# Layer 2's expert blocks: gate and up weights held on TensorE, the turned rows stream

## The reference, cut to what matters

```python
h = silu(einsum('nd,ehd->neh', flat, gate_w)) * einsum('nd,ehd->neh', flat, up_w)
expert_out = einsum('neh,edh->ned', h, down_w)
sel = take_along_axis(expert_out, topk_idx[:, :, None], axis=1)
out = (sel * topk_scores[:, :, None]).sum(axis=1)
out = out + silu(flat @ sgate_w.T) * (flat @ sup_w.T) @ sdown_w.T
```

## Time and profile before

| | |
|---|---|
| median of 3 runs | 3837.25 us (3829.97 to 3837.67) |
| profiled execution | 3835.66 us, its span 3833.8 us |
| the blocks' stretch | first gather at 2457.8 us, last copy of Y at 2690.4 us, next stage from 2693.5 us |
| granted TensorE clock | 0.962 over the span |

### The profile page before, as it was taken

One profiled execution on the slowest core, in us unless ns is written; L12 is line 12 of the kernel. 1 busy time (PEld: TensorE's weight loads), 2 busy tenths in 40 slices (PEclk: granted clock), 3 DMA queues, 4 the chain that ended last, 5 costly groups with the idle time before them and its releaser, 6 DMA issues. The chain is left out here.

```text
span 3833.8 us, 90102 instructions
## 1 busy us (share of the span) xinstructions
PE 3465.1 (90%) x30069; PEld 2574.1 (67%) x30069; DVE 2688.0 (70%) x5870; ACT 2437.2 (64%) x9595; POOL 2075.0 (54%) x2606
## 2 busy tenths in 40 slices
PE   8989979988988999999889998899899998788897
PEld 5656645557776878888666665666688874456587
DVE  6857749977774767777688886644577754979822
ACT  6958944445452437777635991455688875688655
POOL 4534319977993433344366540275666635556744
PEclk9989999999999999999989998999999999999889
DMA  7013420010000000000000003135500003300078
GB/s 110 2 23 48 53 61 1 1 56 1 1 1 22 2 2 7 6 7 6 6 2 6 12 7 119 28 99 91 220 22 21 22 30 116 116 2 10 31 263 302
DMA packets 320103, 185.17 MB, mean 48 GB/s; under 512 B 214104, under 2 KB 289127, under 8 KB 318613
## 3 DMA queue, kind: packets, MB, share of 16 engines
q1 hardware_dynamic: 303716, 147.68, 14.2%
q0 software_dynamic: 13568, 27.36, 3.1%
q10 hardware_dynamic: 2370, 4.39, 0.3%
HBM read 131.43 MB, written 50.54 MB: 47 GB/s over the span
## 5 line engine op out<-in xcount | busy, mean ns | idle before, releaser
L3889 POOL DMA_INDIRECT l2f_b_xb<-l2f_tokens,l2f_inv x160 | 155.5, 972 | 174.8 <-issue 157.9
L2684 POOL TENSOR_TENSOR l1x_Sx<-l1x_Sx,l1x_sm 128x512 f32<-128x512 f32 x128 | 132.6, 1046 | 184.7 <-DVE l1x_sm L2890 184.7
L2684 POOL TENSOR_TENSOR l3a_Sx<-l3a_Sx,l3a_sm 128x512 f32<-128x512 f32 x128 | 133.4, 1043 | 129.8 <-DVE l3a_sm L2890 128.2
L3005 ACT ACTIVATE l1x_Sx<-l1x_Sx,l1x_nmx 128x128 f32<-128x128 f32 x512 | 199.0, 393 | 3.8 <-DVE l1x_nmx L2884 3.8
L1470 PEld LDWEIGHTS l0f_acc<-l0f_d_xk,l0f_d_Z 128*128 128x128 f32 x1024 | 124.7, 191 | 113.8 <-POOL l0f_d_Z L1438 112.8
L3005 ACT ACTIVATE l3a_Sx<-l3a_Sx,l3a_nmx 128x128 f32<-128x128 f32 x512 | 199.0, 392 | 0.1
L865 ACT ACTIVATE l3f_Pr<-l3f_S,l3f_nmx 128x128 f32<-128x128 f32 x512 | 182.5, 402 | 3.3 <-DVE l3f_nmx L795 3.3
L865 ACT ACTIVATE l2x_Pr<-l2x_S,l2x_nmx 128x128 f32<-128x128 f32 x512 | 183.9, 426 | 0.4 <-DVE l2x_nmx L795 0.4
L1350 ACT ACTIVATE l0x_Pr<-l0x_S,l0x_nmx 128x128 f32<-128x128 f32 x512 | 181.4, 403 | 3.1 <-DVE l0x_nmx L1267 2.6
L865 ACT ACTIVATE l0a_Pr<-l0a_S,l0a_nmx 128x128 f32<-128x128 f32 x512 | 182.6, 406 | 0.7 <-DVE l0a_nmx L795 0.7
L1470 PE MATMUL l0f_acc<-l0f_d_xk,l0f_d_Z 128*128 128x128 f32 x1024 | 144.5, 284 | 25.1 <-POOL l0f_d_Z L1438 24.9
(11 more groups left out here) (757 smaller groups left out, 11938.7 us busy)
## 6 DMA issues: line engine op xcount, KB each, us to landing
l3f_b_W<-in_l3f_we SPq DMA_DIRECT2D x72, 514.0 KB, 5.5
l3f_sorted<-l3a_blank SPq DMA_DIRECT2D x1, 17680.0 KB, 51.1
l3x_Mb<-l3x_dram_max SPq DMA_DIRECT2D x32, 512.0 KB, 4.3
l2f_results<-l2f_b_ys SPq DMA_DIRECT2D x40, 256.0 KB, 2.8
l2f_W<-in_l2f_w SPq DMA_DIRECT2D x1, 6144.0 KB, 25.9
l3f_b_xb<-l3f_sorted SPq DMA_DIRECT2D x72, 65.0 KB, 4.4
l0f_ew<-in_l0f_ew SPq DMA_DIRECT2D x1, 4096.0 KB, 13.2
l3f_XS<-l3f_results SPq DMA_DIRECT2D x8, 512.0 KB, 6.6
```

Source lines behind the costliest of these rows:

```text
L2684: pool.tensor_tensor(quad(Sx, s, q), quad(Sx, s, q), bcast_in(sm[:, s, 4 * q:4 * q + 4], P), ALU.mult).then_inc(w_done, 1)
L3005: ins = nc.scalar.activation(Sx[:, s, h, :], Sx[:, s, h, :], ACT.Exp, bias=nmx[:, s, h:h + 1], accum_out=sm[:, s, h:h + 1])
L3889: pool.indirect_dma_start(xb[:, j % 16, :], None, rows[:, :], bass.IndirectOffsetOnAxis(inv[:, j:j + 1], 0), bounds_check=None).then_inc(x ...
```

## The change

The operands of G change places. A ring `wst` of 3 is added in SBUF, 128 x 256 each. VectorE gets a step `weights`: it reads `owner` into a register of its own, and copies the block's gate and up columns into the ring. TensorE holds the ring's gate part, then its up part, and `xT` streams, 128 columns each time, so that G has the hidden width on the partitions. `h` then already lies as `down` needs it: H, its copy, its PSUM bank and `hT` are left out. `product` of block j, which writes `h[j % 2]`, waits for Y of block j-2 where it waited for H of block j-2. `weights` of block j+3 stands ahead of the product of block j+2 in VectorE's loop.

```diff
+        wst = sb("wst", [P, 3, 2 * P])
         h = sb("h", [P, 2, P])
-        hT = sb("hT", [P, 2, P])
...
                 def hidden(j):
-                    if j == blocks - 1:
-                        wait(pe, xt_done, j + 1)
-                    nc.tensor.matmul(G[j % 2][:, 0:2 * P], xT[:, j % 2, :], columns[:, bass.ds(at[j % 4], 2 * P)],
+                    wait(pe, w_done, j + 1)
+                    wait(pe, xt_done, j + 1)
+                    nc.tensor.matmul(G[j % 2][:, 0:P], wst[:, j % 3, 0:P], xT[:, j % 2, :],
+                                     start=True, stop=True)
+                    nc.tensor.matmul(G[j % 2][:, P:2 * P], wst[:, j % 3, P:2 * P], xT[:, j % 2, :],
                                      start=True, stop=True).then_inc(u_mm, 1)
 
-                def turn_hidden(j):
+                def down(j):
                     wait(pe, h_done, j + 1)
-                    wait(pe, ht_done, j)
-                    nc.tensor.transpose(H[:, 0:P], h[:, j % 2, :], C.ident).then_inc(ht_mm, 1)
-
-                def down(j):
-                    if j == blocks - 1:
-                        wait(pe, ht_done, j + 1)
                     wait(pe, y_done, j)
-                    nc.tensor.matmul(Y[:, 0:P], hT[:, j % 2, :], columns[:, bass.ds(at[j % 4] + 2 * P, P)],
+                    nc.tensor.matmul(Y[:, 0:P], h[:, j % 2, :], columns[:, bass.ds(at[j % 4] + 2 * P, P)],
                                      start=True, stop=True).then_inc(y_mm, 1)
...
-                    if 0 <= j + 1 < blocks:
-                        turn_hidden(j + 1)
                     if j >= 0:
                         down(j)
...
                 def product(j):
                     wait(dve, silu_done, j + 1)
-                    wait(dve, ht_mm, j - 1)
+                    wait(dve, y_mm, j - 1)
                     nc.vector.tensor_tensor(h[:, j % 2, :], sg[:, j % 2, :], G[j % 2][:, P:2 * P], ALU.mult).then_inc(h_done, 1)
-
-                def copy_hidden(j):
-                    wait(dve, ht_mm, j + 1)
-                    wait(dve, y_mm, j - 1)
-                    nc.vector.tensor_copy(hT[:, j % 2, :], H[:, 0:P]).then_inc(ht_done, 1)
...
+                def weights(j):
+                    at = dve.value_load(owner[0:1, j:j + 1], min_val=0, max_val=(experts - 1) * width)
+                    wait(dve, u_mm, j - 2)
+                    nc.vector.tensor_copy(wst[:, j % 3, :], columns[:, bass.ds(at, 2 * P)]).then_inc(w_done, 1)
+
+                weights(0)
                 for j in range(-2, blocks):
+                    if j + 3 < blocks:
+                        weights(j + 3)
...
                     if j + 2 < blocks:
                         product(j + 2)
-                    if 0 <= j + 1 < blocks:
-                        copy_hidden(j + 1)
```

More of the change, by code:

```diff
@@ L3871, in gathered_blocks @@
         nth, mine = [sb(nm, [P, NB, experts]) for nm in ("nth", "mine")]
-        T, H, Y, Gs, Us, Ys = [ps(nm) for nm in ("T", "H", "Y", "Gs", "Us", "Ys")]
+        T, Y, Gs, Us, Ys = [ps(nm) for nm in ("T", "Y", "Gs", "Us", "Ys")]
         G = [ps("G0"), ps("G1")]
-        (xt_mm, xt_done, u_mm, silu_done, h_done, ht_mm, ht_done, y_mm, y_done, masked, counted, picked, gu_mm,
-         gate_done, hs_done, ys_mm, xs_done) = sems(17)
+        (xt_mm, xt_done, u_mm, silu_done, h_done, y_mm, y_done, masked, counted, picked, gu_mm,
+         gate_done, hs_done, ys_mm, xs_done, w_done) = sems(16)
         x_in = C.l2f_taken
```

## The result

The kernel after took 3858.42 us (median of 5 runs, 3856.57 to 3859.40) beside 3837.67 us for the kernel before (5 runs, 3829.97 to 3845.99): ratio 1.0051, 95% interval 1.0039 to 1.0062, which is 15 to 24 us slower. The forecast was 3862, in a range of 3840 to 3886.

The account below looks back on a forecast made before the run. TensorE's instruction stream, 1.16 us per block, was taken as the bound; a new ring of 1.39 per block adds +3.4 (last 16), +1.3 (first 18) and +21.5 (middle), +26.2 on 3835.66: 3861.9 us, range 3840 to 3886.

Parts of the forecast that it names:

- The ring: Y(j-2) to product, weights copy, G(j) and Y(j): 2.77 us for two blocks, 1.39 per block; 3862, chance 0.62.
- Y's tail: Ring link on TensorE from Y's weight load to its records' end: 0.49 us.
- Product to copy: Ring link on VectorE, product's start to weights copy's start: 0.95 us, 0.65 for the read and 0.3 for address and waits.
- From the copy's end to Y's weight load: Ring link: 0.12 to wake TensorE and load G's weights, 0.79 with the address load, 0.10 for Y's waits and address.
- Y's end to the product: Ring link from the end of Y(j-2) to the start of product(j): 0.04 us.
- The sum: Added time over the expert blocks: last 16 +3.4, first 18 intervals +1.3, middle +21.5 with nine of eleven paying; together +26.2 us.
- TensorE's own stream after: TensorE's instruction stream without H's turn, if nothing else held it: 1.06 to 1.10 us per block.
- the faster rival: VectorE's address read hides behind the wait for Y(j-2), so no ring limits the blocks: 3827, chance 0.12.
- The port: VectorE's weights copies and GpSimd's gathers hold each other up: 0.00 to 0.05 us per copy counted, at most 0.31.
- the third rival: Port conflict on every weights copy: +0.31 us on the ring, +18 us on top, 3880; chance 0.12.
- The clock: TensorE, less busy, drops to 1.2 GHz, adding some 0.6 us to the ring: +35 us, 3897; chance 0.04.
- the two signs of being wrong: Product still starting as soon as silu is ready, or the step from product to copy under 0.6 us.

Follow-up runs that it names:

- Experiment 6: Kernel before with TensorE's address read taken out, G and Y using the first expert's columns for every block: 3824.37 us, ratio 0.9968.
- Experiments 1: Kernel after with h a ring of 4, so that product(j) waits for Y(j-4) and not Y(j-2): 3844.76 us, ratio 1.0020.
- 2: Kernel after with the weights copy one block earlier, its ring 4 deep, and TensorE waiting for h(j-2) before G(j): 3833.78 us, ratio 1.0001.
- Experiment 3: Kernel after without VectorE's address read, copying the first expert's gate and up columns for every block: 3837.76 us, ratio 1.0011.
- experiment 5: Kernel after with h a ring of 4, weights copied one block earlier into a ring of 4, TensorE waiting for h(j-2): 3833.93 us, ratio 0.9998.
- experiment 7: Kernel after with SyncE reading the address and bringing all three weights by DMA, ring of 8, h ring of 4: 3837.23 us, ratio 1.0001.
- experiment 8: Kernel after with VectorE's address read done twice per block: 3883.16 us, ratio 1.0128.

## Why the prediction was right, point by point

**What bounds the kernel before.** TensorE's instruction stream, 1.16 to 1.18 per block, not its columns. Experiment 6 shows it.

**The ring.** It is there as forecast, from the wait for Y(j-2) to the weights copy and back. Experiments 1 and 2 open it at two different places, and each brings the last 16 blocks back to TensorE's pace. Experiment 3 shortens it by the read, with the same effect. Of its links, the copy (0.29 for 0.28) and Y's tail (0.49) stood as forecast. Product to copy was 0.75 where I took 0.95: the three steps of the read are about the whole of it, and I had added 0.3 for an address and waits that lie beside the read or are short. From the copy's end to Y's weight load it was 0.91 for 1.01. Y's end to the product was 0.11 where I took 0.04: that figure was ScalarE's, for its copy of Y. The sum was 2.55, not 2.77. From its 1.28 per block to the measured 1.33 I take the longer reads behind SyncE's stores, which the forecast left out.

**The sum.** Last 16: +2.2 for +3.4. First 18: +1.1 for +1.3. Middle: +11.1 for +21.5. Here the mis-sized term is the number of blocks that pay. I took nine of eleven. Put by their place in the eleven, 56 of the middle's 124 intervals of T, at five places, went from 85.0 to 97.4 us together, which is 0.22 each and close to the forecast's 0.21. The other 68 are the six behind the one that holds a shared unit's gate and up matmuls, up to two past its down matmuls: 95.4 us before, 94.4 after. So five blocks of eleven paid. The stage cost 14.7 where I had 26.2. The median went up by 20.75. The 6 us between that and the stage are not explained by a cause: the profile puts 5.1 of its own 22.6 ahead of the stage, in code that is the same, and 2.8 behind it. So 3862 was nearer to the result than its working deserves, and that is luck. By the stage alone it would have been 3850.

**TensorE's own stream after.** Forecast 1.06 to 1.10, measured 1.17 (experiments 1 and 5). This term was wrong. The turn left out should give 0.15, and something takes it all. The added waits and the two matmuls where there was one are candidates; no run separates them. It did not show in the result because the ring was longer. For the faster rival it was decisive. Even with the ring open, that rival had nothing to win: experiment 5 stands at 0.9998, not at 3827.

**The port.** Of 160 copies 17 took over 0.33 us, and 11 of these began 0.54 to 0.86 us into a gather. One of them, on the timeline beside GpSimd's gather in the kernel after:

```profile
2543.11 0.95 POOL L3889 DMA_INDIRECT l2f_b_xb<-l2f_tokens,l2f_inv  x1 [0.30 <-PE l2f_b_T L3903]
...
2543.65 0.52 DVE L4030 COPY l2f_b_wst<-l2f_W 128x256 f32 x1 [0.47 <-PE l2f_b_G L3913]
```

It started 0.54 into the gather and ended 0.11 after it, like the pair of the earlier trace rows. The mean copy is 307 ns with a median of 294, so all of this is 160 x 0.013, 2 us. The gathers' mean is 971 ns and their median 945, which is the 0.94 of the earlier trace rows. None of the 73 copies that started in a gather's first half took over 0.32. The Trainium skill's rule (SBUF — State Buffer, "Who interferes with whom"), that the two exclude each other for the whole instruction, would have made the third rival. The traces bear it out only for some of the copies that meet a gather's second half, 11 of 41. (The trap with GpSimd's DMA, which the forecast names beside it, stands on the same page under "SBUF: two separate sides".)

**The marks in the profile.** The pace of the last 16 was 1.33 against a forecast of 1.35 to 1.45. The product's idle time went to Y by half (29.1 of 57.5), not whole. TensorE waited for the copy, in each of the last 16 blocks, but only 7.1 us of it stand in its records, because T's weight load lies in the wait. Gathers still took 0.94 and waited for T, 31.5 us where it was 16.8. The clock was 0.99, so that rival is out. Neither of the two signs of being wrong came: the product waited for Y, and the step from product to copy was 0.75, over 0.6.

## What to carry to other kernels

When a buffer's last reader changes, the wait of its next writer changes with it. Follow what stands behind that writer in program order until the chain comes back, and divide by the blocks that it spans: if that is more than the pace of the busiest stream, a deeper ring or an earlier issue is worth more than the work saved. An address read cost an instruction stream some 0.6 us here, so put it once per block on the engine whose stream has room, and carry everything that depends on it in the same copy. Busy time doesn't show that room: reads and the issue of DMAs don't count as busy, and SyncE's stream was full with them in experiment 7.

## What the runs showed of the hardware

The read of a value into a register held VectorE's stream for some 0.6 us: 305 ns for the load, 190 ns for the register operations (151 on TensorE), 23 ns for the assert, and the gaps between them. From product to copy it was 0.75 with one read, 0.21 with none (experiment 3) and 1.36 with two (experiment 8). A load that began 0.7 to 1.3 us behind the issue of SyncE's store took over 450 ns in all 64 cases of the kernel after, where most others took 300. The longest took 815. In experiment 8 none of TensorE's loads began there, and none of them took that long.

A copy within SBUF took 307 ns for 256 columns and 397 ns for 384. The issue of a DMA with a register's address, 128x384 from SBUF to SBUF, held SyncE's stream for 0.50 us, and together with its read for 1.17 to 1.19 us (experiment 7).
